# Conditioned attention on one core: the embedding's loads and matmuls move into batch 0, and row fills are signalled in two parts

## The reference

```
xn  = layer_norm(x) * norm_w + norm_b
q, k, v = xn @ q_w + q_b, xn @ k_w + k_b, (xn @ v_w + v_b) * mask
att = softmax over the other token of (q . k per head + mask bias)
y   = att @ v
e   = silu(cond) @ emb_w + emb_b              # (8, 512) @ (512, 512): scale | shift, one row per batch
h   = (layer_norm(y) * sb_w + sb_b) * (1 + scale) + shift
out = x + silu(h) @ out_w + out_b
```

## Time and profile before

| | us |
|---|---|
| median of 3 runs | 550.46 (549.0 to 550.89) |
| the profiled execution | 549.22, its span 547.5 |
| TensorE busy / VectorE / ScalarE / GpSimd | 512.8 / 418.6 / 370.7 / 196.0 |
| mean granted TensorE clock | 0.993 of full |

### The profile page before, as it was taken

The page is one execution under the profiler, slowest core; times in us unless marked ns, Lnnn a source line. Parts: engine busy times, 40 slices in busy tenths (PEclk is TensorE's granted clock), DMA queues, the critical chain, the costliest instruction groups (busy, mean ns, idle before and its releaser), DMA issues.

```text
span 547.5 us, 10035 instructions
## 1 busy us (share of the span) xinstructions
PE 512.8 (94%) x2840; PEld 191.4 (35%) x2843; DVE 418.6 (76%) x661; ACT 370.7 (68%) x674; POOL 196.0 (36%) x240
## 2 busy tenths in 40 slices
PE   7698999899999999999999999999999999988796
PEld 3343333233334333433333333433333333422243
DVE  6587777777887878877887878787887878787425
ACT  2305877677867788587867788587867788576751
POOL 4544213425334333425333333425333333124003
PEclk9988999999999999999999999999999999999999
DMA  5633343333324343434424343433324333520011
GB/s 135 219 114 97 98 122 95 110 93 112 115 85 152 106 123 86 137 99 113 116 82 152 106 123 83 136 104 110 117 82 147 107 88 84 161 84 22 1 55 61
DMA packets 55050, 57.95 MB, mean 106 GB/s; under 512 B 12376, under 2 KB 42200, under 8 KB 55024
## 3 DMA queue, kind: packets, MB, share of 16 engines
q1 hardware_dynamic: 54480, 56.84, 35.5%
q10 hardware_dynamic: 544, 0.79, 0.4%
HBM read 36.35 MB, written 21.00 MB: 105 GB/s over the span
## 4 chain that ended last, share of the span: by engine, by line
PE 72%; DVE 9%; issue 7%; ACT 6%; DMA 2%; SPq 2%; ACTq 1%; POOL 0%; DVEq 0%; POOLq 0%
PE pv_ps L511 21%; PE st_ps L492 17%; PE mx_ps L466 11%; PE job_ps L549 8%; DVE negmax L820 7%; ACT probs L644 4%; PE job_ps L556 3%; PE job_ps L569 3%; PE mx_ps L594 2%; PE mx_ps L476 2%; PE mx_ps L599 1%; PE st_ps L410 1%; DMA qk_dram<-qk_parts 1%; ACT h_tanh L692 1%; SPq L1186 1%
## 5 line engine op out<-in xcount | busy, mean ns | idle before, releaser
L820 DVE TENSOR_REDUCE negmax<-mx_ps 128x2 f32<-128x1024 f32 x256 | 301.5, 1220 | 89.6 <-PE mx_ps L466 89.3
L644 ACT ACTIVATE probs<-st_ps 128x512 f32<-128x512 f32 x512 | 278.2, 597 | 115.1 <-PE st_ps L492 112.2
L492 PE MATMUL st_ps<-q_rows,k_rows 115*128 115x512 bf16 x512 | 160.5, 384 | 7.6 <-ACT probs L644 5.1
L511 PE MATMUL pv_ps<-probs,v_rows 128*32 128x512 f32 x1024 | 136.4, 605 | 0.0
L1077 POOL TENSOR_TENSOR qk_rest<-qk_full,qk_parts 128x512 f32<-128x512 f32 x31 | 35.9, 1159 | 223.7 <-ACT qk_parts L656 223.7
L466 PE MATMUL mx_ps<-k_rows,q_rows 51*128 51x512 bf16 x512 | 79.3, 383 | 8.2 <-DMA k_rows<-qk_dram 4.3
L492 PEld LDWEIGHTS st_ps<-q_rows,k_rows 115*128 115x128 bf16 x512 | 39.5, 97 | 113.6 <-ACT probs L644 78.8
L549 PE MATMUL job_ps<-x_norm_t,w_qk 128*128 128x512 f32 x116 | 59.3, 604 | 0.0
L466 PEld LDWEIGHTS mx_ps<-k_rows,q_rows 51*128 51x128 bf16 x512 | 16.9, 94 | 114.7 <-issue 64.3
L1086 POOL TENSOR_TENSOR qk_parts<-qk_rest,qk_parts 128x512 bf16<-128x512 f32 x31 | 36.0, 1160 | 32.5 <-DVE qk_parts L894 20.6
L511 PEld LDWEIGHTS pv_ps<-probs,v_rows 128*32 128x32 f32 x1024 | 20.1, 108 | 34.5 <-issue 30.8
(11 more groups left out here) (112 smaller groups left out, 381.4 us busy)
## 6 DMA issues: line engine op xcount, KB each, us to landing
qk_dram<-qk_parts SPq DMA_DIRECT2D x128, 128.0 KB
q_rows<-qk_dram SPq DMA_DIRECT2D x124, 96.0 KB
k_rows<-qk_dram SPq DMA_DIRECT2D x124, 96.0 KB
x_in<-in_x SPq DMA_DIRECT2D x16, 256.0 KB, 3.0
x_res<-in_x SPq DMA_DIRECT2D x8, 512.0 KB, 3.9
out<-out_sb SPq DMA_DIRECT2D x16, 256.0 KB, 2.6
w_e<-in_L_cond_emb_w SPq DMA_DIRECT2D x1, 1024.0 KB, 5.8
k_rows<-mask_dram SPq DMA_DIRECT2D x64, 6.0 KB
```

What stands on the lines that cost most here:

```text
L492: pe.matmul(st_ps[u % ST_BANKS][:, :], k_rows[0:ROWS_ALL, g, h, c * P:(c + 1) * P], q_rows[0:ROWS_ALL, g, h, :], start=True, stop=True).th ...
L511: mm = pe.matmul(pv_ps[VW * h:VW * (h + 1), :], v_rows[:, c, g * GH + h, :], probs[:, t % P_SLOTS, h, :], start=(c == 0), stop=(c == CH - ...
L644: act.activation(probs[:, t % P_SLOTS, h, :], st_ps[u % ST_BANKS][:, :], ACT.Exp).then_inc(exp_done, 1)
L820: dve.tensor_reduce(by_pair[:, :, j, c], mx_ps[j][:, :, :], AXIS_X, ALU.max, negate=True).then_inc(max_done, 1)
```

## The change

- `w_qk` and the q and k biases count on `qk_loaded`, `w_v` and `vb_row` on `v_loaded`. The first q and k projection waits for the first only.
- The six embedding loads leave the prologue. SP issues them in round 0 behind all of `spread(0, 1, 1)` and ahead of `spread(0, 2, 1)`. They count on `emb_loaded` as before.
- `embedding(0)` and `(1)` run at the end of step 13 of round 0, `(2)` and `(3)` at the end of step 14, into `job_ps`. The first also waits until that bank's q and k projection is read. DVE's part moves to the end of step 15. Job 0 of round 1, in place of the first `pv_step`, waits for `setup_done`.
- Copies 0 to 2 count on `copies_saved`, copy 3 on `rest_saved`. The fills of the own heads' rows go first and wait only for the former. `max_quad` waits for `own_filled`, `st_unit` for `rest_filled`.
- The very first `max_quad` waits for part 0 of group 1 only ahead of its second pair.
- Warm-ups: 4 instead of 10 after step 8; 3 behind each pair of each of the first five `max_quad`s (30) instead of 5 behind each (25).
- DVE's `memset` of `k_rows` moves ahead of `first_parts`; group 1's part 1 (`LATE_FIRST`) moves from step 8 to step 11, behind the first pair of maxima; POOL's `memset` of `v_rows` moves behind `take_part2(-1, 1, 1)`.

```diff
-EMBEDDING_STEP = 11
-WARM_FIRST = {2: 5, 8: 10}
+EMBEDDING_STEP = 13
+WARM_FIRST = {2: 5, 8: 4}
-WARM_MAX = 5
+WARM_MAX = 3
-LATE_FIRST = {(8, 0): ("proj", 1, 1), (14, 1): ("proj", 2, 1)}
+LATE_FIRST = {(11, 0): ("proj", 1, 1), (14, 1): ("proj", 2, 1)}
...
+        def fill_halves(engine, i, halves, n):
+
+            engine.wait_ge(copies_saved, 16 * PARTS * (n + 1))
+            for half in halves:
+                fill_rows(engine, i, half, half)
+            engine.wait_ge(rest_saved, 16 * (n + 1))
+            for half in halves:
+                fill_rows(engine, i, half, 1 - half)
...
                     pe.wait_ge(cond_ready, 1)
                     pe.wait_ge(emb_loaded, EMB_DMAS * 16)
 
+                    pe.wait_ge(*emptied("proj", 2, 1))
                 for k in range(KE):
-                    mm = pe.matmul(pv_ps[:, m * B:(m + 1) * B], w_e[:, k, m * P:(m + 1) * P], cond_t[:, k, :],
+                    mm = pe.matmul(job_ps[:, m * B:(m + 1) * B], w_e[:, k, m * P:(m + 1) * P], cond_t[:, k, :],
...
-                    pe.wait_ge(rows_filled[g], ROW_DMAS * 16 * (mb + 1))
-                    if isinstance(mb, int) and mb == 0 and g == 0:
-
-                        pe.wait_ge(part0_ready, 2)
-                        pe.wait_ge(v_plain_ready, 1)
-                        pe.wait_ge(cond_ready, 1)
+                    pe.wait_ge(own_filled[g], OWN_DMAS * 16 * (mb + 1))
+                first = isinstance(mb, int) and mb == 0
                 for j in range(PAIRS):
+                    if first and step == 0:
+
+                        if j == 0:
+                            pe.wait_ge(xt_ready, KD)
+                            pe.wait_ge(cond_ready, 1)
+                        else:
+                            pe.wait_ge(v_plain_ready, 1)
+                        pe.wait_ge(part0_ready, j + 1)
...
+                    if first and step < MAX_LEAD - 1:
+
+                        keep_warm(st_ps[1], WARM_MAX)
...
+                    pe.wait_ge(rest_filled[g], REST_DMAS * 16 * (b + 1))
...
-                    if isinstance(b, int) and b == 0 and g == 0:
-
-                        pe.wait_ge(setup_done, 1)
...
+                if isinstance(b, int) and b == 1 and t == 0:
+
+                    pe.wait_ge(setup_done, 1)
...
-                    if isinstance(b, int) and b == -1 and 0 <= t - EMBEDDING_STEP < 2 * KD:
-                        embedding(t - EMBEDDING_STEP)
+                    if isinstance(b, int) and b == 0 and 0 <= t - EMBEDDING_STEP < 2:
+                        for k in range(KD):
+                            embedding(KD * (t - EMBEDDING_STEP) + k)
...
                 spread(b, 1, 1, False)
+                if isinstance(b, int) and b == 0:
+                    load_embedding()
                 spread(b, 2, 1, isinstance(b, int) and b == -1)
```

More of the change, by code:

```diff
@@ L386, in copies, with fill_rows @@
             return of if side == 0 else of[:, ::-1]
-        def fill_rows(engine, i, half):
+        def fill_rows(engine, i, half, own):
             at = HALF * half + PARTS
[L391 to L395, removed]
+            heads = slice(PAIRS * own, PAIRS * (own + 1))
+            filled = own_filled[i] if half == own else rest_filled[i]
+            for side, rows in enumerate((q_rows, k_rows)):
+                engine.dma_start(rows[at:at + ROWS_PROD, i, heads, :].rearrange("p h t -> p (h t)"),
+                                 copies(i, side, own, half != own)).then_inc(filled, 16)
+        def fill_halves(engine, i, halves, n):
[5 more added lines that the diff above has]
+                fill_rows(engine, i, half, 1 - half)
         def max_row(g, part):
@@ L1151, in body @@
                 take_part2(b, 1, 1)
+                if isinstance(b, int) and b == -1:
+                    preset_v()
                 if exists(b + 1):
@@ L1199, in _, with load_embedding @@
             sp.dma_start(mask_dram[:, :, :], mask_parts[:, :, :]).then_inc(mask_saved, 16)
+            def load_embedding():
+                with nc.allow_non_contiguous_dma(reason="small vectors, once"):
+                    loads = [(sbw_col[:, :], sb_w.rearrange("(k p) -> p k", p=P)),
+                             (sbb_col[:, :], sb_b.rearrange("(k p) -> p k", p=P)),
+                             (eb_col[:, :], emb_b.rearrange("(k p) -> p k", p=P)),
+                             (ob_row[:, :], out_b.rearrange("(a n) -> a n", a=1).broadcast_to((P, D))),
+                             (w_e[:, :, :], emb_w.rearrange("(k p) n -> p k n", p=P)),
+                             (w_o[:, :, :], out_w.rearrange("(k p) n -> p k n", p=P))]
+                    assert len(loads) == EMB_DMAS
+                    for dst, src in loads:
+                        sp.dma_start(dst, src).then_inc(emb_loaded, 16)
             def spread(b, i, db, turns_first):
@@ L1231, in spread @@
                 if exists(d):
-                    sp.wait_ge(copies_saved, 16 * COPIES * (n + 1))
-                    for half in range(1 if first and i < 2 else 2):
-                        fill_rows(sp, i, half)
+                    fill_halves(sp, i, range(1 if first and i < 2 else 2), n)
             def place_max(b, i):
```

56 lines of the change are left out of this document (26 added, 30 removed).

## The result

| | before | after |
|---|---|---|
| median (5 runs each, side by side) | 549.96 (548.85 to 550.89) | 553.83 (552.96 to 554.54) |
| the profiled execution, its span | 549.22, 547.5 | 554.54, 552.8 |
| mean granted TensorE clock | 0.993 | 0.987 |

The ratio is 1.0074, with a 95% interval of 1.0053 to 1.0094.

The account below looks back on a forecast made before the run. TensorE's own queue was taken to bound the middle batches, VectorE's maxima the prologue from 27.30. Batch 0's 7.7 us lost less the prologue's 5.5 gained made 2.2 slower: 551.4 profiled, 552.7 median, range 549.2 to 555.0.

Parts of the forecast that it names:

- Prologue, 5.5 gained: Prologue: earlier copies and fills 4.6, VectorE's idle 1.3, less 0.4 for a cast; 5.5 us gained (4.4 to 6.2).
- The wait for the loads, 4.9 us: Batch 0, behind step 13's scores: TensorE stands still from 95.5 to 100.4 until w_o lands, 4.9 us.
- The faster rival: Batch 0, at embedding(0)'s wait: w_o lands by 97.4, wait 1.9, clock holds, total 548.5; chance 0.14.
- Thin matmuls less what idle absorbs, 3.2 - 1.6 = 1.6: Batch 0: four embedding columns add 3.2 us on TensorE, of which idle absorbs 1.6 (0.9 to 2.5).
- Half clock, 1.2 us (0 to 2.2): Batch 0, behind the load wait: TensorE falls to half clock for 3.4 us, costing 1.2 (0 to 2.2).
- the 2 us that I had named: Sign for batch 0: the forecast would be wrong if half clock costs over 2 us.
- the distance from the first scores to job 0 of round 1: Sign from the prologue's end through batch 0: this distance, 64.6 us before, should be about 72.
- From round 1 on, nothing: Round 1 onward: TensorE's order is unchanged and the extra rest_filled waits come long after the fills; no cost.
- The new wait in the prologue: Prologue rival: first maxima's second pair waits for group 1's part 0, or its rows come late; 1 to 2 us, 554.2; chance 0.07.

Follow-up runs that it names:

- e3: Kernel after with the six embedding loads, embedding matmuls and VectorE's part back where they were before, keeping the prologue's other edits: 548.01, ratio 0.9971 to before.
- e4: Kernel before with only the embedding moved as in the change (loads, matmuls, VectorE's part, the wait in job 0 of round 1): 558.51, ratio 1.0167.
- e5: Kernel after with the six embedding loads issued by ScalarE in step 8 of the prologue, thin matmuls left in round 0: 552.02, ratio 1.0038 to before.
- e2: Kernel after with 24 warm-up matmuls ahead of TensorE's wait for the embedding loads: 552.94, ratio 1.0068 to before.
- e11: Kernel after with w_e in four 256 KB loads, issued earlier in round 0; w_o and ob_row in place on their own count: 546.76, ratio 0.9954 to before.
- e1: Kernel after with the six embedding loads issued behind spread(0, 0, 1), one group of copies earlier: 551.66, ratio 1.0037 to before.
- e8: Kernel after, loads on ScalarE's queue in the prologue, embedding matmuls at the prologue's end, six more warm-ups: 555.59, ratio 1.0085 to before without the longest run.
- e10: e3 with w_o and ob_row issued in round 0 on their own count, plus warm-ups behind the sixth maxima: 545.85, ratio 0.9931 to before.
- e7: e5 with only the first of each embedding column's four products, and three wide warm-ups ahead of each column: 550.23, ratio 1.0007 to before.

## Why the prediction was right, and where it was off

The direction, the place and the mechanism were as forecast, and the median of 553.83 is 1.1 us above 552.7 and inside the range. The sum against the profiled execution was 2.2 us slower, and 5.3 was measured. By its steps:

- **Prologue, 5.5 gained: right, 5.4 measured.** The third copy and the fills were put at 19.0, and came at 19.11; the first maxima at 22.7, and came at 23.10, since the fills took 3.99 us to be issued and land instead of 3.7. The first scores at 36.9: 36.98. VectorE's idle is gone, and TensorE has full clock from the first maxima to 39.7. By step 13 the gain is 5.8. What I had not seen is which edit makes it. I gave the emptied queue its share of 5.02 us down to 3.2; e3 and e4 show that with the count for own rows nearly all of the gain up to the first maxima is there without it, and about 1 us less up to the first scores.
- **The wait for the loads, 4.9 us: 5.67.** The issue was placed right (87.9 by my sum less the prologue's shift, 88.09 in the trace), and the landing was sized too low: 6.2 and 6.7 us instead of 5.8 and 6.2. The faster rival hoped for a nearly empty DMA there. But the four copies of group 2 are issued right behind the loads, from 89.43, 512 KB as much as the x behind them in the prologue, and the 16 engines were busy for 0.77 of the time from 88.09 to 95.27 (0.87 from 10.93 to 17.60 before). The prediction had asked only whether the loads delay the copies, and not the other way round.
- **Thin matmuls less what idle absorbs, 3.2 - 1.6 = 1.6: 1.80**, by e5's trace, where nothing else disturbs them in batch 0.
- **Half clock, 1.2 us (0 to 2.2): the mis-sized step.** What is left of the 11.0 is 11.0 - 5.67 - 1.80 = 3.5 us. The traces say the same directly: from the first thin block to the second it is 104.64 - 95.36 = 9.28 us here and 100.32 - 94.59 = 5.73 in e5 at full clock, 3.55 apart, and from the second to job 0 both take 7.63. That crosses the 2 us that I had named as the point at which the forecast's reasoning would be wrong, and it is why the distance from the first scores to job 0 of round 1 is 75.3 us and not 72. I had taken the 3.4 us at half that followed the 4.34 us of idle in the old prologue. Here it lasted from 94.3 to 104.5, and nearly all of TensorE's work in it doubled. In the old prologue maxima and wide warm-ups followed the idle; here 16 thin instructions did. e2, e11 and e1 show the clock fall behind or inside a thin block with no more than 0.71 us of idle ahead of it, and before the change the same place, with idles up to 0.71 us too, kept full clock. That speaks for the thin block as a cause of its own. It is not shown. e5's own trace has the same blocks and no fall, and the clock fell where no thin block was near: at 39.7 in the kernel after, behind idles of 0.74, 0.20 and 0.74 us. So why the half clock lasted three times as long as in the prologue stays open; that it did, and what it cost, is shown.
- **From round 1 on, nothing: right.** Job 0 of round 1 shows no idle ahead of it, and the middle batch's window is the same.
- **Rivals.** The new wait in the prologue did not come: ScalarE wrote group 1's part 0 at 22.00, in time. It did come in e1, e5 and e8, where the loads went ahead of something that was needed sooner.

The Trainium skill's page "TensorE: Matmul & The Clock Gate" (section "HAM oscillation") has an array that waits on a DMA start its next tile cold. The trace agrees (0.64 and then 0.50 inside the 5.67 us), and by that rule e2 should have cured it. It cured that fall, but e2's two later falls show that here it is not the whole story.

## What to carry to other kernels

- A bulk load that leaves a crowded place needs a place where nobody behind it is in a hurry, and lead time by its own measured landing (here 6.2 to 6.8 us for 1 MB and what follows it). Ask for each position what is issued next on any queue: rows, 4 KB of maxima and `w_o` itself all waited in turn. Issued in pieces of 256 KB, two behind each of two groups of fills, the same bytes delayed nothing that TensorE waited for.
- When a change has two parts, run each alone. Here the embedding's move added 1 us to what the prologue's other edits gained, and cost eleven in batch 0.
- Price thin matmuls twice, by their length and by a clock that may be low behind them, and put them neither behind a wait nor where every microsecond of TensorE is on the path.

## What the runs showed of the hardware that was not expected

- The granted clock fell behind 16 matmuls of 8 columns with only 0.38 us of idle in the 8 us before (e2), and behind a second such block with 0.71 us (e11).
- It also fell with none near. The wait ahead of the first maxima was 1.79 to 2.44 us in four traces (e5, e8, e1, e10), and the clock fell one to two us behind its end; in seven with 1.33 to 1.71 us it did not, nor in e4 with 2.48.
- The same kernel comes in levels: e3 at 545.2 to 545.4, 547.5 to 548.6 and 549.6 to 550.1, with mean clocks of 0.999, 0.993 to 0.997 and 0.990. So one trace is of one of these levels, and a difference of under 2 us needs many runs: with twelve each, the interval of e5 against e7 is still 1.4 us either way.
- 4 KB issued behind 1.4 MB, 512 KB of x and four copies took 4.4 us (median of two) to land instead of 1.8 (e1), and 2.0 behind 512 KB of `w_e` and the same x and copies (e11).
- The 1 MB of `w_e` took 5.8 us in the prologue, beside other loads, and 6.2 in batch 0.
